# Attention in a fused AdaLN kernel: masks moved from TensorE to VectorE, softmax sums packed by way of DRAM

## The chip, the cores and the metric

One core of a Trainium2 chip runs the whole program in one launch. The metric is device time in microseconds (us). The kernel before takes 953.95 us, the median of three runs (952.17 to 954.7 us). The profiled execution took 952.0 us by the same clock.

## The reference, cut to what matters

Two transformer layers with adaptive layer norm on x of [2, 512, 512], all in float32. The change touches only the attention of layer 0: 32 heads of width 16 over 8 key/value groups (4 heads share a group), causal, on 512 tokens in each of 2 batches.

```python
q = (x @ wq).reshape(b, s, 32, 16)
k = (x @ wk).reshape(b, s, 8, 16); v = (x @ wv).reshape(b, s, 8, 16)
k = jnp.repeat(k, 4, axis=2); v = jnp.repeat(v, 4, axis=2)
scores = jnp.einsum('bihd,bjhd->bhij', q, k) * 16 ** -0.5
scores = jnp.where(tril, scores, finfo.min)
out = jnp.einsum('bhij,bjhd->bihd', softmax(scores), v)
x = x + ga * (out.reshape(b, s, 512) @ wo)
```

Behind it come the expert layer of layer 0 and layer 1, whose matrices are stored as 4-bit codes with scales and are decoded in "pieces" of 128x1024: four curves on ScalarE, three sums on VectorE, a fold on ScalarE, then the scale and an addition. The first six pieces are decoded during the attention.

## The kernel before, in words

All waits between engines are written by hand as semaphores, and each engine runs its own list in program order. The attention runs over 64 units, `n = 4q + ic`. `q` is one of 16 stacks (a batch and a group, with its four heads), `ic` one of four blocks of 128 query rows; under the causal mask unit `ic` has `ic + 1` blocks of 128 keys, so the score rows of one head are 128, 256, 384 or 512 wide.

- SyncE loads a stack with 12 DMAs (`load_stack`, L539, issues at L552 and L558) into one of three buffers, as soon as the transposed scores of the stack three before are done (L548). Its queue also loads the codes and scales of the pieces (L494, L503), at stacks given by `PIECES_AT`.
- TensorE, `scores(n)` (L1599): for each of the four heads one matmul of queries by keys (L1607) into PSUM banks 0 to 3, and a second of 128 columns that adds the mask to the diagonal block (L1609). It goes by halves of two heads: a half of unit n waits until the row maxima of that half of unit n-1 have been read.
- VectorE (L1295): one `reduce_max` for every two heads gives the row maxima MX, two buffers of them. Between units it does the three sums of a piece (L1157) and, for each pair of stacks, the softmax bookkeeping: `copy_odd` (L1215, L1217), `swap_sums` (a shuffle that puts each sum beside its numerator, L1223), two `invert` (reciprocals of 128x256, L1227) and `divide` (L1232). There are 8 pairs.
- GpSimd (L731) writes the maxima as two diagonals into rows 64 to 127 of the stack, so that the next matmul subtracts them. It also scales and adds the pieces (L687, L701), at set units.
- TensorE, `transposed(n-2)` (L1613): keys by queries, now key-major, with the maximum subtracted (L1622), and a mask matmul on the diagonal block (L1625), through banks 4 to 6.
- ScalarE: the exponential of each such block (L879), into ten buffers PT; also the curves (L837), the folds (L846) and a copy of every even stack's result (L566).
- TensorE, `weighted` (L1630, matmuls at L1639): values by exponentials into bank 7, two units at a time at odd n, units n-5 and n-4. The value tile carries columns of ones, so the softmax sums come with the numerators: in every 32 partitions, 16 rows are numerators and 16 are copies of the sum.

Around units 41 to 63 ScalarE and VectorE round and split the finished heads (`ROUND_AT`, `SPLIT_AT`). The output projection (L1661) follows directly on the last `weighted`.

Of the kernel before, what the change touches and what calls it, by code (L numbers as in the profile page):

```python
# [28 lines left out]
P = 128  # L29
# [42 lines left out]
PIECES_AT = {0: (0, 1), 5: (2,), 8: (3,), 11: (4,), 14: (5,)}  # L72
STACKS = 3
RING = 3
# [6 lines left out]
ROUND_AT = {41: 0, 46: 1, 49: 2, 54: 3, 58: 4, 60: 5, 63: 6}  # L81
# [4 lines left out]
STEPS = len(CAPS) + 1  # L86

# [134 lines left out]
def build(nc, a, out):  # L222
# [7 lines left out]
    with ExitStack() as ctx:  # L230
# [18 lines left out]
        GAB = sb("GAB", [P, B, D], F32)  # L249
        MCOL = sb("MCOL", [P, 2, 4, KC, B], F32)  # L250
# [12 lines left out]
        MX = sb("MX", [P, 2, REP], F32)  # L263
# [97 lines left out]

        GD = nc.dram_tensor("gates", (4, B, D), F32, kind="Internal").ap()
# [71 lines left out]
        s_gd = sem("gates_stored")  # L434
        s_gab = sem("gates_spread")
# [102 lines left out]

        def load_stack(sp, n):  # L539
# [67 lines left out]
        def _(sp):  # L607
# [15 lines left out]
            for n in range(B * GROUPS):  # L623
                load_stack(sp, n)
                if n == STACKS:
# [3 lines left out]
                for p in PIECES_AT.get(n, ()):  # L629
                    load_piece(sp, p)  # L630
# [33 lines left out]
        def _(pool):  # L664
# [10 lines left out]
            for odd in range(2):  # L675
                link(nc.gpsimd.memset(V[:, :, odd::2, 1 - odd, :], 1.0))
            pool.wait_ge(s_mm, J["v", B - 1] + 1)
# [41 lines left out]
            for p, n in enumerate(folded[:-1]):  # L719
                for half in range(2):  # L720
                    scale_at[n + 1 + half] = p, half
                    if p >= 2:
                        add_at[(n + 3 if p < 4 else B * GROUPS * TB - 3) + half] = p, half

            for n in range(B * GROUPS * TB):
# [3 lines left out]
                for half in range(2):  # L729
# [3 lines left out]
                                            MX[rows, n % 2].unsqueeze(2).to_broadcast([64, REP, 64]), ALU.mult  # L733
# [35 lines left out]
        def _(act):  # L769
# [98 lines left out]
            for n in range(3):  # L868
# [4 lines left out]
            for n in range(units):  # L873
# [3 lines left out]
                for jc in range(ic + 1):  # L877
# [3 lines left out]
                    done += 1  # L881
                if n % 8 == 5:
                    copy_even(act, n // TB - 1)
                ride(n + 3)
                if step_at(n) and step_at(n)[1] == STEPS - 1:
                    fold(step_at(n)[0])
# [166 lines left out]
        def _(dve):  # L1053
# [174 lines left out]

            def divide(pair):
                b, c = divmod(pair, PAIRS)  # L1230
                cols = slice(b * S, (b + 1) * S)
# [57 lines left out]
            for n in range(B * GROUPS * TB):  # L1289
                for pair in range(2):  # L1290
                    dve.wait_ge(s_s, 2 * n + pair + 1)
                    if n >= 2:
                        dve.wait_ge(s_dg, 2 * (n - 1))
                    w = (n % TB + 1) * P
                    nc.vector.reduce_max(MX[:, n % 2, 2 * pair:2 * pair + 2], PS[:, 2 * pair:2 * pair + 2, 0:w], AX_X  # L1295
                                         ).then_inc(s_mx, 1)
# [4 lines left out]
                if pair_at(n, 4) is not None:  # L1301
                    copy_odd(pair_at(n, 4))
                if pair_at(n, 5) is not None:
                    swap_sums(pair_at(n, 5))
                for half, unit in enumerate((5, 6) if n >= 60 else (7, 8)):
                    if pair_at(n, unit) is not None:
                        invert(half)
                if pair_at(n, 7 if n >= 60 else 9) is not None:
                    divide(pair_at(n, 7 if n >= 60 else 9))
# [186 lines left out]
        def _(pe):  # L1496
# [102 lines left out]
            def scores(n):  # L1599
# [339 lines left out]
```

## Time and profile before

| | |
|---|---|
| time, median of 3 runs | 953.95 us |
| time of the profiled execution | 952.0 us |
| its span | 950.1 us |
| TensorE matmul busy | 877.9 us (92%) |
| VectorE busy | 693.6 us (73%) |
| ScalarE busy | 533.1 us (56%) |
| GpSimd busy | 189.5 us (20%) |
| mean granted TensorE clock | 0.976 of full speed |

The busy time of matmuls is overstated, since their ends are modelled and overlap the next start; distances between starts say more. Line numbers (L1607) are those of the kernel before. The attention lies between the first score matmul at 83.94 us and the first matmul of the output projection at 293.40 us.

### The profile page before, as it was taken

What the parts mean: (1) busy time and instruction counts of PE and PEld (TensorE: products, weight loads), DVE (VectorE), ACT (ScalarE), POOL (GpSimd) and SP (SyncE); (2) the same over time, 40 slices, a digit from 0 to 9 for tenths busy, and PEclk for the clock granted to TensorE, in tenths of its full rate; (3) what the DMA queues carried; (4) which work ended last, traced back from release to release, by engine and by line L of the source; (5) the groups of instructions that cost most, each with busy time, mean ns of one, the idle gap of its engine ahead of it and who ended that gap; (6) DMA issues with size and microseconds to landing.
All of it is one profiled execution on the core that took longest, in us unless ns stands there. A gap on an engine that the chain in (4) does not pass through costs nothing.

```text
span 950.1 us, 13799 instructions
## 1 busy us (share of the span) xinstructions
PE 877.9 (92%) x5224; PEld 693.3 (73%) x5224; DVE 693.6 (73%) x892; ACT 533.1 (56%) x707; POOL 189.5 (20%) x197
## 2 busy tenths in 40 slices
PE   2799999999988889898999999999988999999996
PEld 1567667666667668686888888788866888888885
DVE  3835698888888768778677777587887866667842
ACT  3313667657654434486666657477727766666830
POOL 3002555666557213300000000000040000000004
PEclk9798999999898999999999999999999999999998
DMA  9588565655535103105233333133312333332202
GB/s 309 171 243 152 67 109 69 113 101 66 103 78 179 34 12 105 51 22 147 83 106 103 102 99 113 46 105 95 111 45 67 111 104 97 99 101 67 67 1 89
DMA packets 40610, 93.59 MB, mean 99 GB/s; under 512 B 7000, under 2 KB 10072, under 8 KB 40544
## 3 DMA queue, kind: packets, MB, share of 16 engines
q1 hardware_dynamic: 36416, 87.35, 36.6%
q10 hardware_dynamic: 4128, 5.36, 1.7%
q8 instruction: 42, 0.69, 0.3%
q14 instruction: 24, 0.20, 0.1%
HBM read 77.98 MB, written 2.11 MB: 84 GB/s over the span
## 4 chain that ended last, share of the span: by engine, by line
PE 75%; DVE 9%; issue 5%; POOL 4%; ACT 3%; DMA 2%; SPq 1%; POOLq 0%; DVEq 0%; ACTq 0%
PE PS L1509 15%; PE PS L1510 14%; PE PS L1511 14%; PE PS L1815 5%; PE PS L1814 5%; PE PS L1813 5%; PE PS L1607 4%; PE PS L1639 2%; PE PS L1622 2%; DVE MX L1295 2%; POOL QS L731 2%; DMA WM<-in_WM 1%; POOL X L715 1%; PE PS L1531 1%; DVE ACC L1157 1%
## 5 line engine op out<-in xcount | busy, mean ns | idle before, releaser
L837 ACT ACTIVATE PL<-CODE 128x1024 f32<-128x1024 int32 x200 | 201.9, 1057 | 60.3 <-DVE ACC L1157 55.7
L1509 PE MATMUL PS<-HH,WRH 128*128 128x512 f32 x448 | 176.7, 394 | 11.2 <-DVE HL L1116 4.7
L1510 PE MATMUL PS<-HH,WRL 128*128 128x512 f32 x448 | 175.6, 392 | 0.0
L1511 PE MATMUL PS<-HL,WRH 128*128 128x512 f32 x448 | 175.6, 392 | 0.0
L715 POOL TENSOR_TENSOR X<-X,SCR 128x512 f32<-128x512 f32 x32 | 42.6, 1343 | 560.2 <-DVE SCR L1142 560.1
L1157 DVE SCALAR_TENSOR_TENSOR ACC<-PL,ACC 128x1024 f32<-128x1024 f32 x100 | 123.1, 1231 | 8.4
L879 ACT ACTIVATE PT<-PS 128x512 f32<-128x512 f32 x160 | 85.5, 602 | 67.3 <-PE PS L1622 45.1
L1295 DVE TENSOR_REDUCE MX<-PS 128x2 f32<-128x256 f32 (+3 forms) x128 | 100.5, 820 | 29.4 <-PE PS L1609 14.8
L1509 PEld LDWEIGHTS PS<-HH,WRH 128*128 128x128 f32 x448 | 84.9, 189 | 31.2 <-issue 6.3
L731 POOL TENSOR_TENSOR QS<-ident,MX 64x256 fp32r<-64x256 f32 x128 | 93.6, 732 | 66.6 <-DVE MX L1295 60.0
L1511 PEld LDWEIGHTS PS<-HL,WRH 128*128 128x128 f32 x448 | 84.8, 189 | 18.0
L1510 PEld LDWEIGHTS PS<-HH,WRL 128*128 128x128 f32 x448 | 85.0, 190 | 17.0
L1607 PE MATMUL PS<-KS,QS 128*128 128x128 f32 (+3 forms) x256 | 83.5, 387 | 7.8 <-DVE MX L1295 5.9
L1451 DVE TENSOR_TENSOR HID<-SG,PS 128x512 f32<-128x512 f32 x56 | 37.2, 684 | 69.1 <-PE PS L1511 44.6
L1813 PE MATMUL PS<-WRH,HH 128*128 128x512 f32 x216 | 84.1, 389 | 0.0
L1815 PE MATMUL PS<-WRH,HL 128*128 128x512 f32 x216 | 84.0, 389 | 0.0
L1814 PE MATMUL PS<-WRL,HH 128*128 128x512 f32 x216 | 84.0, 389 | 0.0
L1607 PEld LDWEIGHTS PS<-KS,QS 128*128 128x128 f32 x256 | 50.3, 196 | 30.0 <-DVE MX L1295 18.6
L1157 DVE SCALAR_TENSOR_TENSOR ACC<-PL 128x1024 f32<-128x1024 f32 x50 | 61.5, 1229 | 11.4 <-ACT PL L837 11.3
L846 ACT ACTIVATE ACC<-ACC 128x1024 f32<-128x1024 f32 x50 | 52.9, 1058 | 29.7 <-DVE ACC L1157 29.7
L1622 PE MATMUL PS<-QS,KN 128*128 128x512 f32 x160 | 57.1, 439 | 13.2 <-ACT PT L879 8.2
L1609 PE MATMUL PS<-maskR,padR 128*128 128x128 f32 x256 | 59.1, 240 | 0.0
(225 smaller groups left out, 1528.2 us busy)
## 6 DMA issues: line engine op xcount, KB each, us to landing
CODE<-in_CODES SPq DMA_DIRECT2D x50, 512.0 KB, 3.5
SCALE<-in_SCALES SPq DMA_DIRECT2D x100, 256.0 KB, 4.0
WM<-in_WM SPq DMA_DIRECT2D x12, 1024.0 KB, 5.9
QS<-FH SPq DMA_DIRECT2D x32, 128.0 KB, 4.1
QS<-FL SPq DMA_DIRECT2D x32, 128.0 KB, 5.1
X<-in_X ACTq DMA_DIRECT2D x2, 1024.0 KB, 12.3
GAB<-gates SPq DMA_DIRECT2D x4, 512.0 KB, 3.8
out_x<-X ACTq DMA_DIRECT2D x8, 256.0 KB, 2.0
```

Of the source, the lines that this page charges most:

```text
L731: nc.gpsimd.tensor_tensor(QS[64:P, q % STACKS, :, ic * P + 64 * half:ic * P + 64 * half + 64], ident[rows, rows].unsqueeze(1).to_broadcast ...
L837: nc.scalar.activation(PL[:, n % 3], CODE[:, p % 2], ACT.Prelu, scale=scale, bias=bias, alpha=alpha).then_inc(s_plane, 1)
L879: nc.scalar.activation(block_of(n, jc)[:].rearrange("p h i -> p (h i)"), PS[:, 4 + done % 3], ACT.Exp, scale=HD ** -0.5).then_inc(s_exp, 1)
L1157: nc.vector.scalar_tensor_tensor(acc, PL[:, at_plane % 3], CAPS[i], rest_of, ALU.min, ALU.add).then_inc(s_used, 1)
L1295: nc.vector.reduce_max(MX[:, n % 2, 2 * pair:2 * pair + 2], PS[:, 2 * pair:2 * pair + 2, 0:w], AX_X).then_inc(s_mx, 1)
L1509: nc.tensor.matmul(dst, lh, rh, start=start and k == 0, stop=False)
L1510: nc.tensor.matmul(dst, ll, rh, start=False, stop=False)
L1511: ins = nc.tensor.matmul(dst, lh, rl, start=False, stop=stop and k == KC - 1)
L1607: nc.tensor.matmul(PS[:, h, 0:(ic + 1) * P], QS[:, q % STACKS, h, ic * P:(ic + 1) * P], KS[:, q % STACKS, 0:(ic + 1) * P], start=True, sto ...
L1813: nc.tensor.matmul(dst[t], hh, wh, start=(n == 1 and k == 0), stop=False, skip_group_check=True)
L1814: nc.tensor.matmul(dst[t], hh, wl, start=False, stop=False, skip_group_check=True)
L1815: ins = nc.tensor.matmul(dst[t], hl, wh, start=False, stop=last and n == 1, skip_group_check=True)
```

## The change

Five edits, all in the attention.

1. The mask matmul L1609 goes. VectorE adds a mask tile CMASK (128x512: three blocks of zeros and one of the mask; GpSimd writes it once) in the same instruction that takes the maximum: one `tensor_tensor_reduce` per head instead of one `reduce_max` per two heads. It reads PSUM and CMASK, writes the sum back to PSUM, and puts the maximum into MX. The masks of the transposed scores (L1625) stay.
2. `transposed` runs three units behind instead of two, `weighted` at even n for units n-6 and n-5. MX has three buffers.
3. ScalarE does one curve at a time, each earlier; the fold comes a unit later, and GpSimd scales a piece four units later. Codes and scales of a piece are loaded at separate points.
4. For the first six of the eight pairs, shuffle and reciprocals of 128x512 go. The sums (8 distinct rows of 512) are packed by two DMAs into RC of 128x32, inverted there by one reciprocal, stored to DRAM by two DMAs with the rows swapped, and spread by one DMA into DENS. All five DMAs are in SyncE's queue; the division comes 18 units behind instead of 9. The last two pairs stay as they were, except for their places.
5. MX, RC and CMASK lie where the gates' tile is loaded later.

```diff
-PIECES_AT = {0: (0, 1), 5: (2,), 8: (3,), 11: (4,), 14: (5,)}
+CODES_AT = {0: (0, 1), 4: (2,), 6: (3,), 9: (4,), 12: (5,)}
+SCALES_AT = {0: (0, 1), 5: (2,), 8: (3,), 11: (4,), 13: (5,)}
+MAXIMA = 3
+TURN = 3
+PACK_AT = {2 * pair + 5: pair for pair in range(B * PAIRS - 2)}
+SPREAD_AT = {min(2 * pair + 6, B * GROUPS - 1): pair for pair in range(B * PAIRS - 2)}
 def step_at(n):
-    slots = (2, 4, 6)
+    slots = (0, 4, 6)
...
+        def pack_sums(sp, pair):
+            b, c = divmod(pair, PAIRS)
+            sp.wait_ge(s_odd, 2 * pair + 2)
+            if pair:
+                sp.wait_ge(s_rs, 32 * pair)
+            for u in range(2):
+                sp.dma_start(RC[64 * u:64 * u + 64], DEN[HD * u:P:2 * HD, c, b * S:(b + 1) * S]).then_inc(s_dn, 16)
+        def store_inverses(sp, pair):
+            sp.wait_ge(s_ri, pair + 1)
+            if pair:
+                sp.wait_ge(s_rb, 16 * pair)
+            for u in range(2):
+                sp.dma_start(INV[:, 1 - u], RC[64 * u:64 * u + 64]).then_inc(s_rs, 16)
+        def spread_inverses(sp, pair):
+            sp.wait_ge(s_rs, 32 * (pair + 1))
+            if pair:
+                sp.wait_ge(s_div, pair)
+            sp.dma_start(DENS[:], INV.rearrange("h u s -> (h u) s").unsqueeze(1).to_broadcast([GROUPS, HD, S])
+                         ).then_inc(s_rb, 16)
...
             for n in range(B * GROUPS):
+                if n in PACK_AT:
+                    pack_sums(sp, PACK_AT[n])
+                if n - 1 in PACK_AT:
+                    store_inverses(sp, PACK_AT[n - 1])
                 load_stack(sp, n)
+                if n == B * GROUPS - 1:
+                    store_inverses(sp, PACK_AT[n])
+                if n in SPREAD_AT:
+                    spread_inverses(sp, SPREAD_AT[n])
...
-                    scale_at[n + 1 + half] = p, half
+                    scale_at[n + 5 + half] = p, half
...
             def ride(n):
-                if step_at(n) and step_at(n)[1] < STEPS - 1:
-                    curves(*step_at(n))
+                if step_at(n + 7) and step_at(n + 7)[1] == 0:
+                    curve(step_at(n + 7)[0], 0)
+                if step_at(n + 5) and step_at(n + 5)[1] < STEPS - 1:
+                    p, s = step_at(n + 5)
+                    curve(p, s + 1)
+                if step_at(n - 1) and step_at(n - 1)[1] == STEPS - 1:
+                    fold(step_at(n - 1)[0])
...
+            def invert_packed(pair):
+                dve.wait_ge(s_dn, 32 * (pair + 1))
+                nc.vector.reciprocal(RC[:], RC[:]).then_inc(s_ri, 1)
...
                     dve.wait_ge(s_s, 2 * n + pair + 1)
-                    if n >= 2:
-                        dve.wait_ge(s_dg, 2 * (n - 1))
+                    if n >= MAXIMA:
+                        dve.wait_ge(s_dg, 2 * (n - MAXIMA + 1))
                     w = (n % TB + 1) * P
-                    nc.vector.reduce_max(MX[:, n % 2, 2 * pair:2 * pair + 2], PS[:, 2 * pair:2 * pair + 2, 0:w], AX_X
-                                         ).then_inc(s_mx, 1)
+                    for h in (2 * pair, 2 * pair + 1):
+                        ins = nc.vector.tensor_tensor_reduce(PS[:, h, 0:w], PS[:, h, 0:w], CMASK[:, TB * P - w:], 1.0,
+                                                             MASKED, ALU.add, ALU.max, MX[:, n % MAXIMA, h:h + 1])
+                    ins.then_inc(s_mx, 1)
...
-                if pair_at(n, 4) is not None:
-                    copy_odd(pair_at(n, 4))
...
+                    copy_odd(pair_at(n, 5))
+                if pair_at(n, 9) in PACK_AT.values():
+                    invert_packed(pair_at(n, 9))
+                if pair_at(n, 18) in range(B * PAIRS - 3):
+                    divide(pair_at(n, 18))
+                if n == B * GROUPS * TB - 2:
+                    divide(B * PAIRS - 3)
+                    swap_sums(B * PAIRS - 2)
+                    invert(0)
+                if n == B * GROUPS * TB - 1:
+                    invert(1)
+                    divide(B * PAIRS - 2)
...
-                        nc.tensor.matmul(PS[:, h, 0:(ic + 1) * P], QS[:, q % STACKS, h, ic * P:(ic + 1) * P],
+                        ins = nc.tensor.matmul(PS[:, h, 0:(ic + 1) * P], QS[:, q % STACKS, h, ic * P:(ic + 1) * P],
                                          KS[:, q % STACKS, 0:(ic + 1) * P], start=True, stop=True)
-                        ins = nc.tensor.matmul(PS[:, h, ic * P:(ic + 1) * P], identR, maskR[:], start=False, stop=True,
-                                               skip_group_check=True)
...
-            for n in range(units + 4):
+            for n in range(units + TURN + 2):
                 if n < units:
                     scores(n)
-                if 2 <= n < units + 2:
-                    transposed(n - 2)
-                if n >= 5 and n % 2 == 1:
-                    for unit in (n - 5, n - 4):
+                if TURN <= n < units + TURN:
+                    transposed(n - TURN)
+                if n >= 2 * TURN and n % 2 == 0:
+                    for unit in (n - 2 * TURN, n - 2 * TURN + 1):
                         weighted(unit)
```

## Rows read from the trace of the kernel before

**Rows 1.** Busy time by stretches: start:end, length, then PE, PEld, DVE, ACT, POOL, clock, DMA share, GB/s.
```profile
83.00:279.20 196.20, 179.65 (x1869) 135.84 (x1869) 165.19 (x202) 120.66 (x201) 111.29 (x140) 0.97 0.56 88
279.20:293.40 14.20, 10.18 (x150) 7.30 (x148) 9.76 (x7) 9.14 (x14) 10.76 (x8) 0.76 0.47 133
```

**Rows 2.** Timeline of TensorE, starts of stacks 0, 5, 6, 15 and of the projection.
```profile
83.94 0.33 PE L1607 MATMUL PS<-KS,QS 128*128 128x128 f32 x1 [1.31 <-DVE GR L1287]
...
142.80 0.33 PE L1607 MATMUL PS<-KS,QS 128*128 128x128 f32 x1
...
154.31 0.33 PE L1607 MATMUL PS<-KS,QS 128*128 128x128 f32 x1
...
268.54 0.33 PE L1607 MATMUL PS<-KS,QS 128*128 128x128 f32 x1
...
293.40 0.50 PE L1509 MATMUL PS<-WOH,FH 128*128 128x512 f32 x1
```

**Rows 3.** Timeline of TensorE inside units, for the distances between starts.
```profile
126.08 0.49 PE L1607 MATMUL PS<-KS,QS 128*128 128x512 f32 x1
126.41 0.22 PE L1609 MATMUL PS<-maskR,padR 128*128 128x128 f32 x1
126.47 0.45 PE L1607 MATMUL PS<-KS,QS 128*128 128x512 f32 x1
...
129.54 1.74 PE L1639 MATMUL PS<-PT,V 128*32 128x128 f32 x56
...
132.15 0.91 PE L1622 MATMUL PS<-QS,KN 128*128 128x512 f32 x3
```

**Rows 4.** VectorE groups by shape: count, busy us, mean ns, idle before.
```profile
L1157 DVE SCALAR_TENSOR_TENSOR ACC<-PL,ACC 128x1024 f32<-128x1024 f32 x100 | 123.1, 1231 | 8.4
...
L1295 DVE TENSOR_REDUCE MX<-PS 128x2 f32<-128x1024 f32 x32 | 37.6, 1217 | 1.6 <-POOL QS L731 1.2
...
L1295 DVE TENSOR_REDUCE MX<-PS 128x2 f32<-128x768 f32 x32 | 29.3, 953 | 18.5 <-PE PS L1609 6.4 <-issue 5.9 <-POOL QS L731 3.1
L1227 DVE RECIPROCAL DENS<-DENS 128x256 f32<-128x256 f32 x16 | 27.9, 1744 | 0.1
...
L1295 DVE TENSOR_REDUCE MX<-PS 128x2 f32<-128x512 f32 x32 | 20.7, 686 | 2.3 <-PE PS L1609 1.9
...
L1295 DVE TENSOR_REDUCE MX<-PS 128x2 f32<-128x256 f32 x32 | 12.9, 422 | 7.0 <-PE PS L1609 6.5
...
L1223 DVE STREAM_SHUFFLE DENS<-DEN 128x512 f32<-128x512 f32 x8 | 5.9, 739 | 0.0
```

**Rows 5.** Timeline of VectorE, for distances between neighbouring instructions.
```profile
158.52 1.29 DVE L1295 TENSOR_REDUCE MX<-PS 128x2 f32<-128x512 f32 x2
...
168.83 0.74 DVE L1215 SCALAR_TENSOR_TENSOR NUM<-PS,HALVES,NUM 128x512 f32<-128x512 f32 x1
169.49 0.74 DVE L1217 SCALAR_TENSOR_TENSOR DEN<-PS,HALVES,DEN 128x512 f32<-128x512 f32 x1
...
345.37 0.08 DVE L1356 MATCH_VALUE_LOAD SC<-T,SCO 128x8 f32 x1
345.44 0.21 DVE L1356 MATCH_REPLACE8 SC<-T,SCO 128x64 f32<-128x64 f32 x1
```

**Rows 6.** Timeline of GpSimd: its longest wait for a fold.
```profile
251.78 1.50 POOL L687 TENSOR_TENSOR ACC<-ACC,SCALE 128x512 f32<-128x512 f32 x1 [5.12 <-issue]
```

**Rows 7.** SyncE's DMA queue: timeline of issues, then its waits, then time to landing.
```profile
123.44 1.28 SPq L552 DMA_DIRECT2D QS<-FH  x2
...
132.72 0.59 SPq L558 DMA_DIRECT2D KN<-KL  x1
...
255.95 0.59 SPq L558 DMA_DIRECT2D KN<-KL  x1
...
SPq L552 <- PE PS L1625: 14.8, 8, 3.3
...
KN<-KL SPq DMA_DIRECT2D x32, 32.0 KB, 2.0
```

More of the change, by code:

```diff
@@ L80 @@
 PAIRS = GROUPS // 2
-ROUND_AT = {41: 0, 46: 1, 49: 2, 54: 3, 58: 4, 60: 5, 63: 6}
+ROUND_AT = {41: 0, 46: 1, 49: 2, 54: 3, 58: 4, 61: 5, 63: 6}
 SPLIT_AT = {46: 0, 51: 1, 54: 2, 59: 3}
@@ L249, in build @@
         GAB = sb("GAB", [P, B, D], F32)
+        CMASK = sb("CMASK", [P, TB * P], F32, gab0)
+        RC = sb("RC", [P, S // HD], F32, gab0 + 4 * TB * P)
+        MX = sb("MX", [P, MAXIMA, REP], F32, gab0 + 4 * TB * P + 4 * S // HD)
         MCOL = sb("MCOL", [P, 2, 4, KC, B], F32)
@@ L262, in build @@
         SD = sb("SD", [P, NT], F32)
-        MX = sb("MX", [P, 2, REP], F32)
         HALF = sb("HALF", [P, 2, 4], F32)
@@ L360, in build @@
         XM = [sb(f"XM{n}", [P, 2, D], F32, R0 + off * K) for n, off in enumerate((72, 16, 80, 48))]
+        INV = nc.dram_tensor("inverses", (REP, 2, S), F32, kind="Internal").ap()
         GD = nc.dram_tensor("gates", (4, B, D), F32, kind="Internal").ap()
@@ L434, in build @@
         s_gd = sem("gates_stored")
+        s_dn = sem("denominators_packed")
+        s_ri = sem("denominators_inverted")
+        s_rs = sem("inverses_stored")
+        s_rb = sem("inverses_spread")
         s_gab = sem("gates_spread")
@@ L628, in _ @@
                         sp.dma_start(GD[:, b], MR[b:P:32]).then_inc(s_gd, 16)
-                for p in PIECES_AT.get(n, ()):
-                    load_piece(sp, p)
+                for p in CODES_AT.get(n, ()):
+                    load_codes(sp, p)
+                for p in SCALES_AT.get(n, ()):
+                    load_scales(sp, p)
             sp.wait_ge(s_used, len(CAPS) * N_QKV)
@@ L676, in _ @@
                 link(nc.gpsimd.memset(V[:, :, odd::2, 1 - odd, :], 1.0))
+            pool.wait_ge(s_mm, J["modcol", 1, COLS[-1]] + 1)
+            pool.wait_ge(s_const, 16 * 3)
+            link(nc.gpsimd.memset(CMASK[:, 0:(TB - 1) * P], 0.0))
+            nc.gpsimd.tensor_copy(CMASK[:, (TB - 1) * P:], maskB[:]).then_inc(s_ones, 1)
+            pool.wait_ge(s_ones, 3)
             pool.wait_ge(s_mm, J["v", B - 1] + 1)
@@ L720, in _ @@
                 for half in range(2):
-                    scale_at[n + 1 + half] = p, half
+                    scale_at[n + 5 + half] = p, half
                     if p >= 2:
-                        add_at[(n + 3 if p < 4 else B * GROUPS * TB - 3) + half] = p, half
+                        add_at[(n + 7 if p < 4 else B * GROUPS * TB - 3) + half] = p, half
             for n in range(B * GROUPS * TB):
@@ L732, in _ @@
                                             ident[rows, rows].unsqueeze(1).to_broadcast([64, REP, 64]),
-                                            MX[rows, n % 2].unsqueeze(2).to_broadcast([64, REP, 64]), ALU.mult
+                                            MX[rows, n % MAXIMA].unsqueeze(2).to_broadcast([64, REP, 64]), ALU.mult
                                             ).then_inc(s_dg, 1)
@@ L867, in _ @@
             act.wait_ge(s_free, J["gsum",] + 1)
-            for n in range(3):
+            for n in range(-7, 0):
                 ride(n)
@@ L881, in _ @@
                     done += 1
+                ride(n)
                 if n % 8 == 5:
                     copy_even(act, n // TB - 1)
-                ride(n + 3)
-                if step_at(n) and step_at(n)[1] == STEPS - 1:
-                    fold(step_at(n)[0])
                 if n in ROUND_AT:
@@ L1227, in invert @@
                 link(nc.vector.reciprocal(DENS[:, cols], DENS[:, cols]))
+            def invert_packed(pair):
+                dve.wait_ge(s_dn, 32 * (pair + 1))
+                nc.vector.reciprocal(RC[:], RC[:]).then_inc(s_ri, 1)
             def divide(pair):
                 b, c = divmod(pair, PAIRS)
+                if pair < B * PAIRS - 2:
+                    dve.wait_ge(s_rb, 16 * (pair + 1))
                 cols = slice(b * S, (b + 1) * S)
@@ L1300, in _ @@
                     gate_values()
-                if pair_at(n, 4) is not None:
-                    copy_odd(pair_at(n, 4))
                 if pair_at(n, 5) is not None:
[L1304 to L1309, printed above, removed]
+                    copy_odd(pair_at(n, 5))
[10 more added lines that the diff above has]
+                    divide(B * PAIRS - 2)
                 if n in SPLIT_AT:
```

2 lines of the change are left out of this document (added).

## The prediction

> **What bounds the kernel now.** I read the stretches first, then the timelines of TensorE, VectorE, GpSimd and SyncE's queue, then the groups. The attention up to its last scores is a stretch of 196.2 us, with TensorE's records over 179.7 us of it, VectorE's over 165.2, ScalarE's over 120.7 and GpSimd's over 111.3 [rows 1]. The reader is to see two engines near full, and the others not. An undisturbed stack takes 11.5 us (142.80 to 154.31), but the 15 stacks from the first to the last take 184.6 us, 12.3 each [rows 2]. So 15 x 0.8 = 12 us are stalls. Some 3 us of them are at the first stack, where VectorE computes the gate values; that stays. Others start where GpSimd sits before a scale and waits for a fold, once for 5.1 us [rows 6], and with it the diagonals, the maxima buffer and the scores behind it.
>
> Inside an undisturbed stack TensorE sets the pace. Its starts follow each other without gaps: a 512-wide score matmul and its mask take 0.39 us (126.08 to 126.47), of which the mask's own slot is 0.06; matmuls of 512 columns without a mask follow at (0.91 - 0.45) / 2 = 0.23 us [rows 3].
>
> **TensorE's part.** 256 mask matmuls go. Each frees between 0.06 us (its slot) and 0.39 - 0.23 = 0.16 us (weights that now load behind a longer matmul), so 15 to 41 us; I take 0.12, or 30 us, 1.9 us a stack. TensorE then needs some 9.5 us a stack and no longer sets the pace. What is late next decides.
>
> **VectorE's part.** Reductions of 256, 512, 768 and 1024 elements take 422, 686, 953 and 1217 ns [rows 4]: 1.04 ns an element and 0.157 us fixed. Two of 512 elements take 1.29 us together [rows 5], so the second starts 0.60 us after the first, and the fixed part shrinks to 0.07 us by overlap. A stack has 4 x (128 + 256 + 384 + 512) = 5120 elements in either version, 5.3 us. Before, 8 instructions add 8 x 0.07, in all 5.9 us. After, 16 instructions add 16 f, where f is the fixed part of the new one, which no row shows. Below, f = 0.07, like a reduction. Above, nothing overlaps and the second output costs a small instruction: 0.157 + 0.21 [rows 4, 5] = 0.37. Between them lies the two-source instruction from PSUM: L1217 starts 0.66 us after L1215, so 0.13 fixed; and an operation of two parts, where the load takes a slot of 0.07 to 0.08 ahead of its main part (345.37 to 345.44) [rows 5]. I take f = 0.15, a reduction's 0.07 and 0.08 for the second output, since the new instruction streams from PSUM like the reduction it replaces. Then a stack costs 5.3 + 2.4 = 7.7 us, 1.8 us more, or 29 us over 16 stacks (9 us at f = 0.07, 36 us at 0.18, 85 us at 0.37). A write back to PSUM of what is read there is in no row either; I take it as free, and price the other case below.
>
> By the Trainium skill (VectorE: DVE Perf Modes, section "Two Vector instructions with no wait between them") an instruction that also writes out its accumulator is two, the main one and an accumulator read; no row here shows one. The Trainium skill (Vector Engine (DVE) Microarchitecture Reference, section 5.2) gives about 75 ns of fixed cost per instruction after overlap; the reductions agree with 0.07, L1215 with its 0.13 does not. By these two pages f would be 0.15 as well.
>
> Six pairs lose the shuffle (0.74 us) and two reciprocals (1.74 each) [rows 4]: 6 x 4.2 = 25 us. Each gets one reciprocal of 32 elements: (1744 - 157) / 256 = 6.2 ns an element, 0.36 us, 2 us in all. So VectorE has 29 - 23 = 6 us more work in a stage in which it already had 165 of 196 us [rows 1]. The relief by way of DRAM pays for most of the masks, not for more.
>
> **How they mesh.** In a new stack VectorE's four units cost 1.1, 1.7, 2.2 and 2.7 us. Behind unit 0 comes a curve sum (1.2), but TensorE has three transposed matmuls (0.7) and the long weighted group (1.7 [rows 3]), with gaps some 3.2 us, ahead of the next scores: VectorE idles 1.1 us. Behind unit 1 comes copy_odd (1.4) or the small reciprocal (0.4), behind unit 2 a curve sum (1.2) or a division (0.7); from there TensorE waits for VectorE. The sums are 7.7 + 1.1 + 1.2 + 1.4 + 1.2 = 12.6 us in stacks of one parity and 7.7 + 1.1 + 1.2 + 0.4 + 0.7 = 11.1 in the other, 11.9 on average. The last scores' stack then starts at 83.9 + 15 x 11.9 + 3 = 265.4 us, against 268.5.
>
> **The queues.** SyncE loads stacks 5 to 15 between 123.44 and 256.54 us [rows 7], 133.1 us. Its waits in the stage are 14.8 us [rows 7], of which I put 12 in this stretch; the rest, 121 us, is issuing, at 0.63 us a DMA (0.59 and the gap) and more where it is held up. The change puts 27 DMAs into this stretch before stack 15 is complete: 6 x 2 packs, 5 x 2 stores, 5 spreads, 17 us. The trigger comes one unit later, some 1.5 us. So the last stack is issued at the earliest at 123.4 + 1.5 + 121 + 17 = 263, and has landed 2.0 us later [rows 7], at 265 us. What is queued behind each new wait is the next stack: the pack waits for copy_odd, the store for the reciprocal, and TensorE waits for the stack. Both waits are met about when the stack's own trigger comes, so I cost them at nothing; late, each is paid in full. The division comes 9 units after the reciprocal, which covers two DMA trips. So VectorE and SyncE's queue allow the same 265 us, 3.2 us earlier than now.
>
> **The rest.** Folds a unit later and scales four units later take away GpSimd's waits; that is counted, since my 11.9 has no stall in it. Single curves fit in ScalarE's 60% load. GpSimd's diagonals have three buffers, so its load of 111 us in 196 is covered. The end, 268.54 to 293.40, is 24.9 us now [rows 2]. A further unit is transposed after the last scores (0.5 to 1.5 us), and VectorE has 0.7 + 0.7 + 1.7 us between the last two units instead of 1.7; against that stand the lost stalls of the last stack (TensorE's clock is 0.76 behind it [rows 1]). I take no change, 2 us either way. Behind the attention nothing changes.
>
> Sum: 952.0 - 3.2 = 948.8 us for an execution like the profiled one (span 950.1 and 1.9 around it). The median of the runs is 1.95 above that execution, so 950.7; I say 950.5 us.
>
> **Rivals.**
> - *Full overlap.* f is 0.07 to 0.1, and the hold-ups in the queue (9.9 us a stack for 12 DMAs, where 12 x 0.63 is 7.6) shrink by half, 11 x 1.2 = 13 us. Then VectorE needs 11.0 us a stack, and the last starts at 83.9 + 165 + 3 = 252 us: 16 us earlier, 937 us; with one of the two only in part, 943. For it: the reductions do overlap to 0.07. Against it: the queue's loads were as long when nothing else was in it. I take 940.
> - *VectorE becomes the bound and costs more (the other side).* The place is the new instruction. From f = 0.165 on the change loses, since 11.9 + 16 x 0.015 = 12.1 us is what a stack takes now beside the 3 us at the start. With L1215's 0.13 and 0.08 for the second output, f = 0.21: 12.9 us a stack, the last starts at 280 us, 12 us later, 965 us. For it: L1215 is the row that has PSUM and a second tensor like the new one.
> - *The new instruction runs at half rate*, because it reads and writes a PSUM bank at once: 5.3 us a stack more, 16 x 5.3 = 85 us, some 1035 us. Against it: 1024 elements from two SBUF tensors take 1231 ns [rows 4], full rate. The Trainium skill (Vector Engine (DVE) Microarchitecture Reference, section 7) warns that a two-tensor instruction with two non-bf16 SBUF sources halves the throughput, for want of a port for the accumulator's readback; the trace disagrees where no accumulator is read, and shows none that does.
> - *The queue is late.* Each pack or store that waits holds the next stack; 1 us in each of 11 stacks brings the last one to 276, 962 us, and TensorE idles before each stack, where its clock may fall.
>
> **How the numbers follow.** Forecast 0.42, with its own range 945 to 955; full overlap 0.22; costlier instruction 0.26; late queue 0.07; half rate 0.03. A difference of 0.3% (2.9 us) is about what can be told from no change: the forecast gives 0.27 faster and 0.15 same, the rival above 0.22 faster, the others slower but for 0.03 of the late queue. That is faster 0.49, same 0.18, slower 0.33. The range 938 to 967 leaves out the half rate and the tails.
>
> **What would show it.** After: L1609 gone; VectorE busy over 90% of the stage, the new instructions some 0.15 us plus 1.04 ns an element apart (f is read there); scores waiting for VectorE, not GpSimd; the queue's waits for transposed scores gone and DMA waits before the first scores of late stacks; no wait of 3 us at the scale. Wrong I would be if the new instructions stand 0.2 us or more beyond their elements, or if the last stack starts before 258 us.

## The result, and the profile after

The change makes the kernel slower: 967.3 us (median of 4 runs, 966.5 to 967.5) against 953.1 us for the kernel before, measured beside it; the ratio is 1.0165, with a 95% interval of 1.0144 to 1.0187. The forecast was 950.5 us, and the time lies just above the range given (938 to 967). The profiled execution has a span of 965.6 us, 15.5 us above that of before.

Two stretches of the kernel after, which answer to [rows 1] (columns as there; the second ends at the projection):

```profile
83.00:293.30 210.30, 173.10 (x1612) 121.15 (x1613) 160.73 (x559) 120.06 (x199) 113.46 (x140) 0.85 0.55 89
293.30:307.00 13.70, 10.79 (x151) 7.72 (x149) 12.07 (x16) 10.14 (x16) 5.54 (x7) 0.75 0.45 128
```

VectorE is busy for 160.7 of 210.3 us, 76% where the prediction looked for over 90%, and TensorE's granted clock is 0.85, where it was 0.97. Neither engine is full. The time went into waits and into a low clock.

TensorE's starts, which answer to [rows 2]: stacks 5, 6, 9, 15 and the projection.

```profile
146.66 0.41 PE L1678 MATMUL PS<-KS,QS 128*128 128x128 f32 x2 [0.66 <-DVE MX L1361]
...
158.82 0.41 PE L1678 MATMUL PS<-KS,QS 128*128 128x128 f32 x2 [1.22 <-DVE MX L1361]
...
198.38 0.41 PE L1678 MATMUL PS<-KS,QS 128*128 128x128 f32 x2 [0.76 <-DVE MX L1361]
...
282.74 0.41 PE L1678 MATMUL PS<-KS,QS 128*128 128x128 f32 x2 [0.76 <-DVE MX L1361]
...
306.94 0.50 PE L1580 MATMUL PS<-WOH,FH 128*128 128x512 f32 x1
```

The 15 stacks take 282.74 - 83.56 = 199.2 us, 13.3 each; before they took 184.6, and the forecast had 181.5. The last stack starts 14.2 us later than before. What lies behind is timed by one matmul of the stage that follows the projection, the one that waits 3.00 us for VectorE in both kernels, here of the kernel before and then of the kernel after:

```profile
336.17 0.50 PE L1509 MATMUL PS<-HH,RQH 128*128 128x512 f32 x1 [3.00 <-DVE HL L1116]
```
```profile
352.11 0.50 PE L1580 MATMUL PS<-HH,RQH 128*128 128x512 f32 x1 [3.00 <-DVE HL L1173]
```

It comes 67.6 us after the last stack's start before, and 69.4 us after it now; 14.2 + 1.8 is the 15.5 us of the span within half a microsecond. The 1.8 us lie behind the attention: from the last stack's start to the projection it is 24.2 us (24.9 before), but from there to this matmul 45.2 us (42.8 before). In that stretch TensorE stands idle 2.37 us once (1.63 before), and the granted clock over the 6 us around it is 0.72, where it stayed at 1.00 before. So nearly all of the loss lies in the stacks, and the head of one shows it. TensorE in stack 9:

```profile
199.58 0.44 PE L1678 MATMUL PS<-KS,QS 128*128 128x128 f32 x2 [0.79 <-DVE MX L1361]
199.85 0.68 PE L1691 MATMUL PS<-QS,KN 128*128 128x512 f32 x2
200.37 0.40 PE L1694 MATMUL PS<-padR,maskR 128*128 128x512 f32 x1
200.70 3.21 PE L1708 MATMUL PS<-PT,V 128*32 128x128 f32 x56
203.84 0.88 PE L1678 MATMUL PS<-KS,QS 128*128 128x256 f32 x4
```

TensorE waits 0.76 us for the maxima of the unit before and does two score matmuls. It waits 0.79 us again and does the other two and the transposed matmuls of one unit. Then its long weighted group (56 matmuls, L1708) takes 3.21 us, where the same group took 1.74 before [rows 3]. The granted clock over the stretches of such a group in stack 9 and in stack 5, and over the 2.3 us ahead of the first:

```profile
198.40:200.70 2.30, 1.51 (x8) 0.95 (x8) 2.27 (x13) 0.30 (x1) 0.95 (x2) 1.00 0.96 98
200.70:203.90 3.20, 3.20 (x58) 2.79 (x57) 1.35 (x1) 1.73 (x3) 3.02 (x3) 0.51 0.66 87
```
```profile
147.86 0.44 PE L1678 MATMUL PS<-KS,QS 128*128 128x128 f32 x2 [0.79 <-DVE MX L1361]
...
148.97:150.70 1.73, 1.73 (x58) 1.53 (x57) 0.00 (x0) 1.73 (x3) 1.51 (x3) 1.00 0.91 98
```

At 0.51 the long group ran at 1.2 GHz, and the clock fell just behind the two waits; the one in stack 5 ran at 2.4 GHz, and that stack took 12.2 us. Yet in stack 5, as in stack 15, the same two waits stand ahead of the group (0.66 and 0.79 us, 0.76 and 0.80). So the waits don't bring the low clock every time, and what decides is not shown here. Of the 13 long groups ahead of the last stack 12 took 2.3 to 3.2 us, in all 15 us above 1.74.

VectorE stands idle meanwhile:

```profile
200.52 1.53 DVE L1214 SCALAR_TENSOR_TENSOR ACC<-PL,ACC 128x1024 f32<-128x1024 f32 x1
204.52 0.43 DVE L1361 CUSTOM_DVE_ANT_0 PS<-PS,CMASK 128x256 f32<-128x256 f32 x1 [2.47 <-PE PS L1678]
```

The groups of VectorE in 83 to 293 us, which answer to L1295 in [rows 4], put 36.7 of its 49.6 us of idle time at this unit (256 elements, a record for each head):

```profile
L1361 DVE CUSTOM_DVE_ANT_0 PS<-PS,CMASK 128x512 f32<-128x512 f32 x60 | 39.6, 722 | 9.6 <-PE PS L1678 4.7 <-issue 3.6 <-DVE NUM L1295 1.4
L1361 DVE DVE_READ_ACCUMULATOR2_ANT MX<- 128x1 f32 x252 | 35.4, 140 | 0.0
L1361 DVE CUSTOM_DVE_ANT_0 PS<-PS,CMASK 128x384 f32<-128x384 f32 x64 | 33.6, 588 | 1.2 <-PE PS L1678 1.0
L1361 DVE CUSTOM_DVE_ANT_0 PS<-PS,CMASK 128x256 f32<-128x256 f32 x64 | 25.2, 456 | 36.7 <-PE PS L1678 36.7
L1361 DVE CUSTOM_DVE_ANT_0 PS<-PS,CMASK 128x128 f32<-128x128 f32 x64 | 17.7, 322 | 1.4 <-PE PS L1678 1.1
```

The price of the new instruction is read from neighbouring starts, as in [rows 5]:

```profile
198.09 0.73 DVE L1361 CUSTOM_DVE_ANT_0 PS<-PS,CMASK 128x512 f32<-128x512 f32 x1
198.74 0.14 DVE L1361 DVE_READ_ACCUMULATOR2_ANT MX<- 128x1 f32 x1
198.74 0.73 DVE L1361 CUSTOM_DVE_ANT_0 PS<-PS,CMASK 128x512 f32<-128x512 f32 x1
...
199.63 0.33 DVE L1361 CUSTOM_DVE_ANT_0 PS<-PS,CMASK 128x128 f32<-128x128 f32 x1
199.88 0.14 DVE L1361 DVE_READ_ACCUMULATOR2_ANT MX<- 128x1 f32 x1
```

512 elements start 0.65 us apart and 128 elements 0.25 us, so f = 0.65 - 512 x 0.00104 = 0.12 us. The records show it as two instructions, a main part and a read of the accumulator (140 ns), and the read begins with the next main part. It costs next to nothing: L1217, which has two sources and no accumulator, has 0.13 us of fixed part [rows 5]. The new instruction runs at full rate with its result written back to the PSUM bank that it reads. By the Trainium skill (VectorE: DVE Perf Modes, section "Two Vector instructions with no wait between them") it would be two instructions: the trace agrees.

SyncE's queue has waits, but no score matmul waits for a DMA in this stage:

```profile
SPq L591 <- PE PS L1694: 10.9, 5, 7.7
...
SPq L560 <- DVE DEN L1274: 5.0, 4, 1.6
SPq L568 <- DVE RC L1288: 3.4, 2, 3.0
```

### The profile page after: what moved, and what is told of

Its sections match the earlier page's. It is cut to its first block, busy times and chain, and to the rows that moved or that the text cites. A ratio compares the mean times of both kernels' runs of the same rounds, so it can differ in the third digit from the quotient of the medians.

```text
span 965.6 us, 13701 instructions
## 1 busy us (share of the span) xinstructions
PE 873.9 (91%) x4968; PEld 681.0 (71%) x4968; DVE 692.8 (72%) x1258; ACT 533.7 (55%) x707; POOL 190.3 (20%) x199
## 4 chain that ended last, share of the span: by engine, by line
PE 61%; DVE 6%; ACT 3%; issue 2%; POOL 1%; DMA 1%; POOLq 0%; SPq 0%; DVEq 0%; ACTq 0%
PE PS L1580 13%; PE PS L1581 13%; PE PS L1582 13%; PE PS L1883 5%; PE PS L1884 5%; PE PS L1882 5%; PE PS L1708 1%; POOL X L769 1%; DVE ACC L1214 1%; DVE PS L1361 1%; PE PS L1865 1%; PE PS L1853 1%; PE PS L1620 1%; DVE SCR L1199 1%; DVE ST L1141 1%
## 5 line engine op out<-in xcount | busy, mean ns | idle before, releaser
L1361 DVE CUSTOM_DVE_ANT_0 PS<-PS,CMASK 128x128 f32<-128x128 f32 (+3 forms) x256 | 117.8, 522 | 49.0 <-PE PS L1678 43.5
L1678 PE MATMUL PS<-KS,QS 128*128 128x128 f32 (+3 forms) x256 | 68.8, 377 | 33.6 <-DVE MX L1361 30.8
L1678 PEld LDWEIGHTS PS<-KS,QS 128*128 128x128 f32 x256 | 42.9, 210 | 61.5 <-DVE MX L1361 29.4
L1708 PE MATMUL PS<-PT,V 128*32 128x128 f32 x1280 | 58.2, 348 | 0.0
## 6 DMA issues: line engine op xcount, KB each, us to landing
X<-in_X ACTq DMA_DIRECT2D x2, 1024.0 KB, 12.2
```

Source lines behind the costliest of these rows:

```text
L1361: ins = nc.vector.tensor_tensor_reduce(PS[:, h, 0:w], PS[:, h, 0:w], CMASK[:, TB * P - w:], 1.0, MASKED, ALU.add, ALU.max, MX[:, n % MAXIM ...
L1678: ins = nc.tensor.matmul(PS[:, h, 0:(ic + 1) * P], QS[:, q % STACKS, h, ic * P:(ic + 1) * P], KS[:, q % STACKS, 0:(ic + 1) * P], start=Tru ...
```

## The experiments

The theory after this reading: the new instruction is cheap enough, and the failed term is VectorE's idle time behind unit 0. Its cause is either the place of the long group (between the scores of units 0 and 1) or the clock behind TensorE's waits. Rivals: VectorE's load, the queue.

**1. The parts of the change.** The kernel before with edit 1 alone:

```diff
-                    nc.vector.reduce_max(MX[:, n % 2, 2 * pair:2 * pair + 2], PS[:, 2 * pair:2 * pair + 2, 0:w], AX_X
+                    for h in (2 * pair, 2 * pair + 1):
+                        ins = nc.vector.tensor_tensor_reduce(PS[:, h, 0:w], PS[:, h, 0:w], CMASK[:, TB * P - w:], ...
```

> The kernel before with edit 1 alone: no score mask matmuls, the mask added by VectorE in the instruction that takes the maximum; order, softmax sums, curves as before. In the trace of the changed kernel this instruction stands 0.65 us apart at 512 elements and 0.25 us at 128, so its fixed cost is 0.12 us and VectorE does 5.3 + 16 x 0.12 = 7.2 us a stack instead of 5.9, 21 us more in all, here without the relief of the packed sums. Theory A (VectorE and TensorE now alternate, and TensorE's clock drops in the waits): slower than before by 10 to 25 us, 963 to 978 us. Rival B (the loss comes from the DMAs in SyncE's queue or from the later order, not from the masks): faster than before, 935 to 950 us, since 30 us of TensorE's work are gone.

Measured: 958.8 us, ratio 1.0062 (1.0041 to 1.0083), 12.7 us a stack: between the two theories. Every long group among the stacks that the records show whole, but for the last stack's, is at 1.74 us. TensorE's scores wait for VectorE, which here has no relief by packed sums (the weight loads' waits stand in the first row, the matmuls' in the second):

```profile
PEld PS L1617 <- DVE MX L1304: 43.2, 59, 2.3
PE PS L1617 <- DVE MX L1304: 25.8, 48, 1.9
```

The converse, the kernel after without edit 1 (`reduce_max` and the mask matmuls back):

> The changed kernel without edit 1: reduce_max for two heads and the mask matmuls as before, everything else changed (three units behind, single curves, packed sums by way of DRAM). Theory A: TensorE sets the pace again at 11.5 us a stack, now without the 9 us of stalls at the folds, so 943 to 948 us, and the clock stays near 1.0. Rival B (queue or order cost the time): 960 us or more.

Measured: 955.1 us, ratio 1.0028 (1.0013 to 1.0044), 12.2 us a stack, all but one long group at 1.74 us. The expectation was too low. VectorE has less to do, and yet it waits for scores, most of all at unit 1 behind the long group (23.1 of the 42.4 us).

```profile
DVE MX L1358 <- PE PS L1676: 42.4, 42, 2.9
```

The kernel before with edit 3 alone (single curves earlier, folds and scales later):

```diff
-                    scale_at[n + 1 + half] = p, half
+                    scale_at[n + 5 + half] = p, half
```

> The kernel before, with edit 3 alone (single curves earlier, folds a unit later, scales and additions four units later, codes and scales loaded apart). Theory A (the stalls of 12 us over 15 stacks in the kernel before are GpSimd's waits for folds): those waits vanish, a stack takes 11.5 to 11.8 us, 943 to 948 us. Rival B (the stalls have several causes, and another takes the place): 950 to 953 us.

Measured: 951.0 us, ratio 0.9991 (0.997 to 1.0012), no difference that can be told. GpSimd's waits for folds are gone from the stacks (one of 5.2 us stands behind the last scores) and the last stack starts at 263.9 us, 4.7 us earlier, not the 9 to 12 us that I had put down to them.

**2. The place of the long group.** The kernel after, with weighted at odd n, so that the long group lies behind the scores of unit 3:

```diff
-            for n in range(units + TURN + 2):
+            for n in range(units + 4):
...
-                if n >= 2 * TURN and n % 2 == 0:
-                    for unit in (n - 2 * TURN, n - 2 * TURN + 1):
+                if n >= 5 and n % 2 == 1:
+                    for unit in (n - 5, n - 4):
```

> The changed kernel with the weighted groups at odd n, units n-5 and n-4, as in the kernel before, so that the long group (units 2 and 3 of a stack) is issued behind the scores of unit 3, where VectorE has its longest maxima, and no longer behind the scores of unit 0, where it has its shortest. Theory A (the place of the long group makes VectorE wait 2.4 us at every unit 1 and TensorE wait at unit 0, where its clock then falls): 943 to 955 us. Rival C (VectorE's own work is the bound whatever the place): within 3 us of the changed kernel, 964 to 970 us. Rival D: the exponentials of the last unit are not ready one unit later, and TensorE waits for ScalarE instead: 960 us or more with waits for PT.

Measured: 951.8 us, ratio 0.9998 (0.9978 to 1.0019), 15.5 us below the kernel after. Every long group that the records show whole is at 1.74 us. But now the mechanism of the queue step appears, with a wait for copy_odd beside it (DEN is what copy_odd writes, KN what a stack's loads bring):

```profile
PEld PS L1708 <- DVE DEN L1274: 15.3, 6, 3.1
...
PEld PS L1678 <- DMA KN<-KL: 11.5, 7, 3.0
```

Changing the place takes the whole loss away, but this run moves order and clock together. Two more tried what is left. With copy_odd one unit earlier (`pair_at(n, 4)`):

> The kernel after, with the long weighted group at odd n (units n-5, n-4) and copy_odd one unit earlier. Theory A (the place of the weighted group is the failed term; what was left in the run that moved it alone is the wait of the short weighted group for copy_odd, 13 to 17 us over 7 groups, partly hidden): 943 to 948 us, the waits of L1708 for L1274 gone, and the queue's lateness (DMA waits of the scores) the next in line. Rival B (the queue already holds the stacks at 12.1 us each): 950 to 954 us, DMA waits grown by what the waits for copy_odd lose.

Measured: 952.9 us, ratio 1.0019 (0.9997 to 1.0042): the rival's case. The waits for copy_odd fell, and those for KN rose to 17.8 us, which speaks for the queue as what holds the stacks; experiment 3 tests it. The same kernel with the masks back on TensorE:

> The kernel after, with the masks back on TensorE (one reduce_max for two heads), the weighted group at odd n and copy_odd one unit earlier. Theory A (the even place of the weighted group cost the kernel with masks back 7 to 10 us, as it cost the kernel after 15): 943 to 948 us against 955 at the even place. Rival B (with masks on TensorE the place doesn't matter, since TensorE sets the pace by its own work): 953 to 956 us. If A holds and the time is at or below that of the same kernel with masks on VectorE, the move of the masks brings nothing by itself at either place.

Measured: 950.1 us, ratio 0.9994 (0.9975 to 1.0013). Against 955.1 at the even place that is 5 us by the medians, with the masks on TensorE too. The intervals of the two ratios just touch, and copy_odd moved with the order, so the order's own share is not shown here.

**3. The queue.** The kernel with odd weighted and earlier copy_odd, the five DMAs of a pair in ScalarE's queue:

```diff
+PACK_N, STORE_N, SPREAD_N = 11, 15, 17
... (the same calls leave SyncE's queue)
+                for at, do in ((PACK_N, pack_sums), (STORE_N, store_inverses), (SPREAD_N, spread_inverses)):
+                    if n >= at and (n - at) % 8 == 0 and (n - at) // 8 < B * PAIRS - 2:
+                        do(act, (n - at) // 8)
```

> Like the kernel with weighted at odd n and copy_odd earlier, and the five pack, store and spread DMAs of a pair issued from ScalarE's queue instead of SyncE's. Theory A (SyncE's queue, filled by these DMAs, sets when late stacks begin, as the queue step of the prediction has it): DMA waits of the scores gone, a stack takes 11.3 to 11.7 us, 938 to 946 us. Rival B (the waits for copy_odd and for the reciprocal now hold ScalarE's exponentials, or VectorE is the bound at 12 us anyway): 948 to 955 us.

Measured: 938.6 us, ratio 0.9875 (0.9844 to 0.9905): the fastest version, 11.4 us a stack on average. Some waits for KN are left in it (9.1 us of the weight loads'). Its shortest stack, 8, takes 10.0 us, and the one behind it 12.0:

```profile
175.94 0.71 PE L1674 MATMUL PS<-KS,QS 128*128 128x128 f32 x4
...
185.96 0.76 PE L1674 MATMUL PS<-KS,QS 128*128 128x128 f32 x4
```

The same move in the kernel after, at the even place:

> The kernel after, with the five pack, store and spread DMAs in ScalarE's queue and nothing else changed (the long weighted group stays at even n). Theory A (in the kernel after the queue is not late, since a stack takes 13.3 us and no score waits for a DMA; the place of the long group is the cause): 965 to 968 us. Rival B (the queue's delays act through the packing and the division, so that relief of it alone brings most of the 14 us that it brought at odd n): 952 to 958 us.

Measured: 968.2 us, ratio 1.0175 (1.0138 to 1.0211). At 13.1 us a stack no score matmul waits for a DMA, with the five DMAs in either queue, so the relief brings nothing. And the 938.6 us kernel with the masks back on TensorE:

> The kernel with everything that has helped (weighted at odd n, copy_odd earlier, the five DMAs in ScalarE's queue, 938.6 us) and the masks back on TensorE, with one reduce_max for two heads. Theory A (with the stalls gone, TensorE's 11.5 us a stack is the bound with masks, and VectorE's 11.3 without, so edit 1 is worth about nothing to 5 us by itself): 938 to 944 us. Rival B (edit 1 is the gain, once order and queue let it work): 946 to 950 us, 11.8 to 12 us a stack. Rival C (edit 1 costs even here): 930 to 936 us.

Measured: 944.4 us, ratio 0.9924 (0.9899 to 0.995), between the theories: by the medians edit 1 is worth 5.7 us there, though the intervals of the two ratios overlap by a little. The same with weighted one unit at a time (`weighted(n - 5)` at every n):

> The 938.6 us kernel with weighted one unit at a time, unit n-5 at every n, instead of two at odd n. Theory A (the size of TensorE's work between two score groups is what makes VectorE wait, so that smaller, even groups shorten the waits of 18.6 us that are left): 932 to 937 us. Rival B (the longest single unit, 16 blocks of 4 matmuls, now falls behind the scores of unit 0, where VectorE has the least to do, as in the kernel after): 940 to 946 us.

Measured: 945.1 us, ratio 0.9934 (0.9913 to 0.9955). The largest unit's group again falls behind the scores of unit 0, and TensorE's waits for maxima grow to 29.7 us (weight loads) and 20.1 us (matmuls), from 19.1 and 7.9.

**4. The clock by itself.** First, the kernel after with the 256 mask matmuls kept beside the new instruction (the masks are added twice):

> The changed kernel with the score mask matmuls kept as well (the mask is then added twice). They serve only as work for TensorE, 0.06 to 0.16 us each, 256 of them. If the low TensorE clock in the long weighted group of every stack (3.2 us where it took 1.7 before) is what costs, the clock recovers and the time falls to 950 to 960 us although TensorE does more. If the cause is only the order of waits between TensorE and VectorE, the added work lies partly on the path: 967 to 975 us.

Measured: 966.9 us, ratio 1.0158 (1.0121 to 1.0195). This looks like the end of the clock theory, but it decides nothing. The clock rose from 0.84 to 0.90 in 84 to 276 us and the long groups' excess over 1.74 us fell from 15 to 7 us, so 8 us came back. The rest of the 15 stacks grew by as much, from 184 to 192 us. The cause is, I take it, the 256 matmuls (15 us by the slot of [rows 3]), since they stand between the scores that VectorE waits for. So matmuls were repeated only where TensorE waits anyway:

```diff
+                        for _ in range(4 if ic == 0 and half == 0 and n > 0 else 0):
+                            nc.tensor.matmul(PS[:, h, 0:P], QS[:, q % STACKS, h, 0:P], KS[:, q % STACKS, 0:P],
+                                             start=True, stop=True)
                         ins = nc.tensor.matmul(PS[:, h, 0:(ic + 1) * P], ...
...
+                    for _ in range(4 if ic == 0 and n > 0 else 0):
+                        nc.tensor.matmul(dst, KN[q % STACKS][:, 0:P], QS[:, q % STACKS, :, 0:P], start=True, stop=True)
                     ins = nc.tensor.matmul(dst, KN[q % STACKS][:, jc * P:(jc + 1) * P], ...
```

> The kernel after, with matmuls repeated in place, results the same, where TensorE waits for the maxima of unit 3: four more of the transposed matmul of unit 0 (0.9 us) and four more of each of the first two score matmuls of unit 0 (0.5 us). The order is unchanged; only the two waits of some 0.8 us are filled. Theory A (the clock falls to 1.2 GHz because of these waits, and the long group at that clock, 1.15 us a stack longer on average over the 13 slow or partly slow stacks, is what makes a stack 13.3 us): the long group back at 1.74 us in most stacks, 12.2 to 12.5 us a stack, 952 to 958 us. Rival B (the order is what costs, and the low clock follows from the waits without prolonging the chain): 965 to 970 us, whatever the long group takes.

Measured: 954.8 us, ratio 1.003 (1.0013 to 1.0047). TensorE in stack 5, where the repeats (L1679) stand between the scores (L1681):

```profile
142.81 0.61 PE L1679 MATMUL PS<-KS,QS 128*128 128x128 f32 x4
143.25 0.61 PE L1681 MATMUL PS<-KS,QS 128*128 128x128 f32 x3
...
144.54 1.74 PE L1713 MATMUL PS<-PT,V 128*32 128x128 f32 x56
146.21 0.74 PE L1681 MATMUL PS<-KS,QS 128*128 128x256 f32 x4
```

With 1.4 us more work a stack and the same order the kernel is 12.5 us faster, and every long group among the stacks is at 1.74 us. The second of the two waits is gone in every stack; the first is gone in stack 5, 0.34 us in stacks 4 and 6, and up to 1.9 us in later ones, where it is mostly a wait for KN, that is, for the queue. More work and less time leave no cause for the gain but the clock: the low clock is the cause of most of the loss. Next the repeats with the queue relieved, and the repeats in the 938.6 us kernel:

> The kernel after, with both the repeated matmuls (954.8 us alone) and the five DMAs in ScalarE's queue (968.2 us alone): the long weighted group stays at even n. Theory A (the low clock is the first bound of the kernel after and the queue the second, which only shows once the clock is back; the even place costs nothing by itself): 938 to 944 us, 11.3 to 11.7 us a stack, DMA waits of the scores gone. Rival B (at the even place VectorE's waits of 30 us stay, and the queue waits of 11.7 us turn into these): 950 to 955 us.

> The 938.6 us kernel (weighted at odd n, copy_odd earlier, DMAs in ScalarE's queue) with the same repeated matmuls. Theory A (its clock is 0.96 in the stage and its long groups are at 1.74 us already, so there is nothing to give back, and 1.4 us a stack of repeats lie in what were waits): 937 to 942 us. Rival B (the repeats are on the path when the waits are small): 945 to 955 us. If A, the repeats cost next to nothing, and what they brought in the kernel after is the clock alone.

Measured: 952.1 us, ratio 0.9993 (0.9979 to 1.0008), and 953.6 us, ratio 1.0012 (0.9999 to 1.0025). In both there are stacks of 11.6 to 11.7 us that TensorE's records fill but for 0.4 to 0.6 us, so the repeats themselves had become its limit there; they cost the 938.6 us kernel 15 us. Hence two runs with fewer of them, queue relieved: only the four repeats of the transposed matmul, then two.

> The kernel after with the five DMAs in ScalarE's queue and four repeats of the transposed matmul of unit 0 only (0.9 us a stack); the repeats of score matmuls (0.5 us) are left out. Theory A (in the 952 us run with all repeats TensorE ran without gaps at 11.7 us a stack, so the repeats themselves were its bound, and the even place costs little by itself once the clock holds): 0.5 us a stack less, 943 to 947 us, if four repeats are enough to hold the clock. Rival B (the even place is the bound through VectorE's waits): 950 to 953 us. Rival C (the clock falls again, since the wait between the two halves is open): 958 to 966 us, long groups above 1.74 us.

> As the kernel with four repeats of the transposed matmul, but with two (0.45 us a stack). Theory A (shorter repeats, same clock): 2 to 7 us below the kernel with four, 937 to 944 us. Rival B: the same as with four, 950 to 953 us. Rival C (two repeats do not hold the clock): 960 to 968 us, most long groups at 2.7 to 3.2 us.

Measured: 951.4 us, ratio 1.0008 (0.9983 to 1.0032), and 955.1 us, ratio 1.0054 (1.003 to 1.0077); the second lies between the rival's 950 to 953 us and the 960 to 968 us of a clock that falls. The same kernel without repeats took 968.2 us, so four of them bring 16.7 us and two 13.1 us. With either number 12 of the 14 long groups behind scores of unit 0 take 1.74 us, the other two 2.8 to 3.2 us. TensorE in a stack of the second:

```profile
190.65 0.41 PE L1674 MATMUL PS<-KS,QS 128*128 128x128 f32 x2 [0.29 <-DVE MX L1357]
191.85 0.44 PE L1674 MATMUL PS<-KS,QS 128*128 128x128 f32 x2 [0.79 <-DVE MX L1357]
192.13 0.67 PE L1689 MATMUL PS<-QS,KN 128*128 128x512 f32 x2
192.64 0.40 PE L1692 MATMUL PS<-padR,maskR 128*128 128x512 f32 x1
192.96 1.74 PE L1706 MATMUL PS<-PT,V 128*32 128x128 f32 x56
194.63 0.62 PE L1674 MATMUL PS<-KS,QS 128*128 128x256 f32 x3
```

and VectorE behind it:

```profile
195.17 0.43 DVE L1357 CUSTOM_DVE_ANT_0 PS<-PS,CMASK 128x256 f32<-128x256 f32 x1 [0.84 <-PE PS L1674]
```

This is stack 9 of above with the first wait filled from 0.76 to 0.29 us: the same order, the long group at full clock, and VectorE's wait 0.84 instead of 2.47 us. Removing half of the repeats brought nothing further. What is left at the even place (951 to 955 us against 938.6) I put down to the order: TensorE still waits for unit 3's maxima and VectorE for unit 1's scores (19.2 us up to the last stack). No run separates that from the repeats' own time, the two slow groups, or copy_odd, which is a unit earlier in the 938.6 us kernel.

## Why the prediction was wrong

*The failed step* is "How they mesh", and in it one number: "three transposed matmuls (0.7) and the long weighted group (1.7 [rows 3]), with gaps some 3.2 us", so that "VectorE idles 1.1 us". I took the group's 1.74 us from [rows 3], a trace in which the group stands behind the scores of unit 3 and always ran at full clock, for a kernel in which I myself had made it wait: "from there TensorE waits for VectorE". The waits come just ahead of the long group; in 12 of 13 stacks its clock falls to 1.2 GHz for all or part of it, it takes 2.3 to 3.2 us, and VectorE idles 2.3 to 3.9 us. That is 15 of the 17.7 us by which the 15 stacks missed the forecast; by experiment 12.5 us, and 13.1 to 16.7 us with the queue relieved, net of what the repeats cost. With the clock held the mean of the step is right: stacks 3 to 8 of the run with two repeats take 11.6 to 12.2 us (forecast 11.1 and 12.6 in turn, mean 11.9). VectorE's wait is 0.84 us (forecast 1.1) where a curve sum lies behind unit 0. The step had one there in every stack. Every fourth step of a piece is a fold on ScalarE and no sum, and a stack with the fold there waits some 2.2 us even at full clock, as stack 5 of the kernel after does. A fall of the clock stood in the prediction only under the late queue, which did not happen. Neither of its two signs of being wrong came (an instruction of 0.2 us or more beyond its elements, a last stack before 258 us): both looked elsewhere.

*A smaller miss* of 2.7 us is what is left of several. With the long groups' excess taken off, stacks 9 to 14 together take 5.0 us more than at 11.9 us a stack, and stacks 2 to 8 together 1.6 us more, while the first two take 3.9 us less than the forecast with its 3 us. Late stacks take longer at full clock too (13.2 us for stacks 11 and 13 of the run with two repeats). VectorE also splits heads from stack 11 on, and the 11.9 had none of that; no run isolates it.

*TensorE's part* (30 us freed, about 9.5 us a stack): near. TensorE's records cover 9.3 to 9.7 us in stacks 4, 5, 8 and 9 of the 938.6 us kernel, at a granted clock of 1.00. But freed time in an engine that then waits was here worth less than nothing.

*VectorE's part*: f is 0.12, where 0.15 was taken; 7.2 us a stack for the maxima where 7.7 was forecast. The half rate did not come, and the costlier instruction (965 us for f = 0.21) would have given nearly the right time for the wrong reason. That the packed sums carry their part is likely, but not shown by itself: the kernel before with the masks alone is 0.6% slower than it, while with packed sums, the later transposed unit, single curves and the DMAs elsewhere the masks gain 5.7 us. (At f = 0.18 and 0.37 the step's sum gives 37 and 86 us, not 36 and 85.)

*The queue*: not late in the kernel after, as forecast, and its limit shows about where the step said it would, at some 12.2 us a stack (the runs at 951.8 and 952.9 us; its 265 us for the last stack allowed 11.9). Moving the DMAs is worth 14 us there and nothing at 13.3 us a stack.

*The rest*: the end, from the last stack's start to the projection, shrank by 0.7 us, within the 2 allowed. "Behind the attention nothing changes" did not hold in the profiled execution: 2.4 us more up to the matmul at 352.11, beside the low clock shown above. The fold stalls went, but were worth 4.7 us of stage and no measurable time, less than I counted.

What stays open: why the clock stays up behind the same two waits in stacks 5 and 15, how the even place's remaining 13 to 16 us split between the waits, the repeats and copy_odd's place, and whether the clock and the order share some of the 15 us at the odd place.

## What to carry to other kernels

When a change takes work from an engine and makes it wait, don't price its next long group from a trace in which it never waited: look what stands right behind the new wait, and price it at the lower clock too. Put the longest group of a filled engine where it would wait for the other one, not where the other one has the least to do. Here a move paid only once another had made way: the queue's relief was worth nothing at the even place (968.2 us) and 14 us at the odd one (938.6 us), and the masks cost time alone (958.8 us) and gained 5.7 us in the best kernel. So a part that tests neutral alone isn't shown to be worthless.

## What the hardware showed that I had not expected

- Extra matmuls can make a kernel faster: with 0.45 us a stack of repeats ahead of the first wait 12 of 14 long groups ran at 1.74 us (968.2 to 955.1 us), and with 1.4 us a stack the kernel after went from 967.3 to 954.8 us.
- The clock of a stage (0.85) hides where it falls: in stack 9 it was 1.00 over the matmuls between the waits and 0.51 over the group behind them, and all that stood idle ahead of it were two waits of 0.76 and 0.79 us with two matmuls between them.
- `tensor_tensor_reduce` with a PSUM source, written back to the same bank, costs, from start to start, 1.04 ns an element and 0.12 us, its accumulator read included; that record of 140 ns overlaps the next instruction.
